# Second output projection, weight split and first routed tiles in one phase; routed tiles without a loop on TensorE

## The reference, cut to what matters

```python
# layer 0: 8 experts, 2 per token; layer 1: 16 experts, 4 per token
def step(acc, inputs):
    w1e, w2e, ce = inputs
    h = xt @ w1e                      # 256 -> 2 * 176
    a, b = jnp.split(h, 2, axis=-1)
    y = jax.nn.silu(a) * b @ w2e      # 176 -> 256
    return (acc + ce[:, None] * y, None)
...
out = jnp.einsum('bhqk,bkhd->bqhd', attn, V).reshape(B, S, D)
return out @ Wo.T + bo                # second output projection
```

## Time and profile before

| | |
|---|---|
| time, median of 3 runs | 2127.53 us |
| time of the profiled execution | 2133.09 us |
| its span | 2130.9 us |
| TensorE busy | 1723.5 us (81%), 10296 matmuls |
| VectorE, ScalarE, GpSimd busy | 1387.3, 946.3, 672.5 us |
| granted TensorE clock over the span | 0.92 of full speed |
| HBM read, written | 144.97 MB, 141.82 MB |

### The profile page before, as it was taken

The page is one execution under the profiler, slowest core; times in us unless marked ns, Lnnn a source line. Parts: engine busy times, 40 slices in busy tenths (PEclk is TensorE's granted clock), DMA queues, the critical chain, the costliest instruction groups (busy, mean ns, idle before and its releaser), DMA issues. The chain is left out here.

```text
span 2130.9 us, 36160 instructions
## 1 busy us (share of the span) xinstructions
PE 1723.5 (81%) x10296; PEld 1331.0 (62%) x10297; DVE 1387.3 (65%) x2825; ACT 946.3 (44%) x2201; POOL 672.5 (32%) x850
## 2 busy tenths in 40 slices
PE   3999985638892780899999999995688988879997
PEld 2877874428881560455555555543588888868886
DVE  4589996315564876977777777723455656546766
ACT  0455652313343651166666656663333434333343
POOL 1455621730006824044343434340000000027760
PEclk9999997869995895899999999998899999989999
DMA  6445523623333996235353535317633333356661
GB/s 224 156 125 172 152 43 84 223 87 96 104 99 119 321 352 191 69 97 134 93 138 90 145 82 148 82 49 208 187 96 103 103 99 110 99 177 191 200 191 53
DMA packets 288496, 292.61 MB, mean 137 GB/s; under 512 B 122665, under 2 KB 245034, under 8 KB 286300
## 3 DMA queue, kind: packets, MB, share of 16 engines
q1 hardware_dynamic: 265340, 236.62, 37.9%
q0 software_dynamic: 18432, 50.36, 7.5%
q10 hardware_dynamic: 4608, 4.20, 0.6%
HBM read 144.97 MB, written 141.82 MB: 135 GB/s over the span
## 5 line engine op out<-in xcount | busy, mean ns | idle before, releaser
L1473 ACT ACTIVATE ca_PT<-ca_psS 128x512 f32<-128x512 f32 (+3 forms) x768 | 344.9, 493 | 273.1 <-PE ca_psS L1508 259.7
L1399 DVE TENSOR_REDUCE ca_part<-ca_psM 128x1 f32<-128x512 f32 (+3 forms) x608 | 368.5, 656 | 85.3 <-PE ca_psM L1493 60.7
L1508 PE MATMUL ca_psS<-ca_QS,ca_KS 128*128 128x512 f32 (+3 forms) x768 | 306.1, 409 | 4.1 <-ACT ca_PT L1473 4.1
L801 POOL DMA_INDIRECT g_y<-ys_scratch,pos x128 | 130.7, 1021 | 501.9 <-POOLq L68 456.5
L1486 PE MATMUL ca_psM<-ca_KS,ca_QS 126*128 126x512 f32 (+3 forms) x768 | 247.1, 365 | 15.9 <-issue 13.7
L1508 PEld LDWEIGHTS ca_psS<-ca_QS,ca_KS 128*128 128x128 f32 x768 | 147.7, 195 | 106.4 <-ACT ca_PT L1473 101.3
L776 DVE TENSOR_TENSOR f_x_lo<-f_psT,f_x_hi 128x256 fp32r<-128x256 f32 x214 | 90.9, 425 | 162.2 <-ACT f_x_hi L755 157.6
L755 ACT ACTIVATE f_x_hi<-f_psT 128x256 fp32r<-128x256 f32 x214 | 82.3, 385 | 248.0 <-PE f_psT L708 247.7
L708 PE MATMUL f_psT<-ident,f_xs 128*128 128x128 f32 x428 | 89.2, 293 | 113.8 <-issue 56.9
L719 PE MATMUL f_psU<-ffn_hi,f_x_hi 128*128 x428 | 164.8, 385 | 1.0 <-DVE f_x_lo L776 1.0
L1486 PEld LDWEIGHTS ca_psM<-ca_KS,ca_QS 126*128 126x128 f32 x768 | 141.4, 194 | 37.4 <-DVE ca_part L1399 14.3
(11 more groups left out here) (258 smaller groups left out, 4386.6 us busy)
## 6 DMA issues: line engine op xcount, KB each, us to landing
f_xs<-xs_scratch SPq DMA_DIRECT2D x214, 128.0 KB, 2.0
ys_scratch<-f_ys SPq DMA_DIRECT2D x214, 128.0 KB, 1.7
xs_scratch<-fa_blank SPq DMA_DIRECT2D x32, 640.0 KB, 4.0
ca_QS<-qk_scratch SPq DMA_DIRECT2D x32, 512.0 KB, 6.7
ca_KS<-qk_scratch SPq DMA_DIRECT2D x32, 512.0 KB, 8.1
po_raw<-in_ffn SPq DMA_DIRECT2D x24, 608.0 KB, 4.8
xs_scratch<-fa_blank SPq DMA_DIRECT2D x32, 384.0 KB, 3.4
v_scratch<-gp_v_st SPq DMA_DIRECT2D x32, 256.0 KB, 3.8
```

The costliest lines, as they stand in the source:

```text
L801: pool.indirect_dma_start(dst[:, k, :], None, y_dram, bass.IndirectOffsetOnAxis(pos[:, tile, k:k + 1], 0)).then_inc(got, 16)
L1399: dve.tensor_reduce(dst, psM[(slot * NU + u) % SLOTS][:, 0:nh * w].rearrange("p (h k) -> p h k", h=nh), AX.X, ALU.max)\
L1473: act.activation(PT[:, s % 2, h, off:CHUNK], psS[(GH * s + h) % SLOTS][:, off:CHUNK], ACT.Exp)\
L1508: pe.matmul(psS[tile % SLOTS][:, off:CHUNK], KS[:, slot, h, kt * P:(kt + 1) * P], QS[:, slot, h, c * CHUNK + off:(c + 1) * CHUNK], start=T ...
```

## The change

1. `sparse_experts` (both layers use it before, the first layer after): TensorE's program is written out for all tiles instead of looping. `load_owners` is gone; `load_owner` loads one tile's expert number with one TENSOR_LOAD, once a step, between `up` and `transpose_h`. ScalarE, VectorE and SP keep their loops.
2. In the second layer `project_out` and `sparse_experts` are replaced by one phase, `project_beside_experts`. A step n, for n from 0 to 15, loads and splits expert n's weights, projects the attention's tiles 2n and 2n + 1, and carries the routed tiles, two steps later than the loads of the same step: `transpose` of tile n - 2, `up` of tile n - 3, `transpose_h` of n - 4, `down` of n - 5. From step 16 on only routed tiles are left. An `up` of one of the first 16 tiles waits for the split of the expert of its own number (a tile's expert never has a higher number). TensorE is written out here too; the others write out 24 steps and loop over the rest.
3. The projection's tiles have two staging buffers (`OB`) instead of four and share the PSUM buffers `psT` and `psY` with the routed tiles, which take turns in a fixed order (`turns_T`, `turns_Y`).
4. `mean_rstd`, `logits`, `before`, `every` and `tile_ids` are freed before this phase, which makes room for its buffers.

```diff
-def in_steps(eng, *stages, tiles=TILES, first=None, begin=None):
+def in_steps(eng, *stages, tiles=TILES, first=None, beside=None):
...
     whole = tiles // POS_TILES
-    if begin:
-        begin(0, first)
     for n in range(first):
+        if beside is not None:
+            beside(n)
         step(n)
     with eng.Fori(first // POS_TILES, whole) as b:
-        if begin:
-            begin(b * POS_TILES, POS_TILES)
         for i in range(POS_TILES):
             for lag, stage in stages:
                 back = -(-(lag - i) // POS_TILES) if lag > i else 0
                 stage(b * POS_TILES + (i - lag), (i - lag) % POS_TILES, b - back if back else b)
-    if begin:
-        begin(whole * POS_TILES, tiles + most - whole * POS_TILES)
     for n in range(whole * POS_TILES, tiles + most):
         step(n)
...
@@ -688,17 +684,11 @@
         def _(pe):
             owners = {}
 
-            def load_owners(n, count):
-                before = 0 if isinstance(n, int) and n == 0 else 3
-                count = min(count + before, NT - n + before) if isinstance(n, int) else count + before
-                _, values = nc.values_load_multi_w_load_instructions(te[0:1, bass.ds(n - before, count)], (pe.engine,), min_val=0, max_val=E - 1,
+            def load_owner(t, i, b):
+                _, values = nc.values_load_multi_w_load_instructions(te[0:1, t:t + 1], (pe.engine,), min_val=0, max_val=E - 1,
                                                                       skip_runtime_bounds_check_because="a count of ends, cut to E - 1 where it is written")
-                owners.clear()
-                owners.update({j - before: v for j, v in enumerate(values)})
-
-            def owner(i, lag):
-
-                return owners[(i + lag) % POS_TILES - lag]
+                owners.clear() if t == 0 else owners.pop(t - 4, None)
+                owners[t] = values[0]
 
...
             def up(t, i, b):
-                e = owner(i, 1)
+                e = owners[t]
...
             def down(t, i, b):
-                e = owner(i, 3)
+                e = owners[t]
...
                 ins.then_inc(down_done, 1)
-            in_steps(pe, (0, transpose), (1, up), (2, transpose_h), (3, down), tiles=NT, begin=load_owners)
+            for n in range(NT + 3):
+                for lag, stage in ((0, transpose), (1, up), (0, load_owner), (2, transpose_h), (3, down)):
+                    if lag <= n < NT + lag:
+                        stage(n - lag, (n - lag) % POS_TILES, (n - lag) // POS_TILES)
...
+def project_beside_experts(nc, tag, o_tile, s_dram, wo_dram, bo_dram, w_dram, E, NT, te, w_hi, w_lo, xs_dram, ys_dram, ident):
+
+    XR, YR, RAW, OB, SB = 4, 4, 2, 2, 4
+    LAG, PAIR = 2, TILES // E
+    FIRST = POS_TILES * -(-(E + 2) // POS_TILES)
+
+
+
+    def projected(n):
+        return range(PAIR * n, PAIR * (n + 1)) if 0 <= n < E else ()
...
+        h = sb("h", [P, 2, MID])
+        h_hi, h_lo = sb("h_hi", [HALF, 2, 2 * P], F32R), sb("h_lo", [HALF, 2, 2 * P], F32R)
+        wo, bo = sb("wo", [P, KT, HID]), sb("bo", [P, HID])
+        raw = sb("raw", [P, RAW, WE])
+        o_st, oT, s_sb = sb("o_st", [P, OB, HID]), sb("oT", [P, 2, HID]), sb("s_sb", [P, SB, HID])
+        psT, psU, psH, psY = ps("psT"), ps("psU"), ps("psH"), ps("psY")
+        wo_in, bo_in, oT_done, oT_out, s_done, s_out, hiw_done, low_done = (
...
+
+        turns_T, turns_Y = [], []
+        for n in range(NT + LAG + 4):
+            turns_T += [("o", t) for t in projected(n)] + [("x", n - LAG)] * (0 <= n - LAG < NT)
+            turns_Y += [("o", t) for t in projected(n - 1)] + [("x", n - LAG - 3)] * (0 <= n - LAG - 3 < NT)
+        place_T, place_Y = ({x: k for k, x in enumerate(turns)} for turns in (turns_T, turns_Y))
+        assert all(place[k, t] % 2 == t % 2 for place in (place_T, place_Y) for k, t in place if k == "x")
...
+            def beside(n):
+                if n >= E:
+                    return
+                if n >= RAW:
+                    sp.wait_ge(low_done, n - (RAW - 1))
+                sp.dma_start(raw[:, n % RAW, :], w_dram[n]).then_inc(raw_in[n % RAW], 16)
+                for t in projected(n):
+                    if t >= OB:
+                        sp.wait_ge(oT_done, t - (OB - 1))
+                    src = o_tile(t)
+                    sp.dma_start(o_st[:, t % OB, :].rearrange("p (g n) -> p g n", g=src.shape[1]), src).then_inc(staged[t % OB], 16)
+            sp.dma_start(wo[:], wo_dram).then_inc(wo_in, 16)
+            sp.dma_start(bo[:], bo_dram.partition_broadcast(P)).then_inc(bo_in, 16)
+            in_steps(sp, (0, load), (LAG + XR + 1, store), tiles=NT, first=FIRST, beside=beside)
+            for i in range(YR):
+                sp.wait_ge(stored[i], 16 * len(range(i, NT, YR)))
...
+            def load_owner(t, i, b):
+                _, values = nc.values_load_multi_w_load_instructions(te[0:1, t:t + 1], (pe.engine,), min_val=0, max_val=E - 1,
+                                                                      skip_runtime_bounds_check_because="a count of ends, cut to E - 1 where it is written")
+                owners.clear() if t == 0 else owners.pop(t - 4, None)
+                owners[t] = values[0]
+
+            def free(turns, at, x_out, o_out):
+                if at >= 2:
+                    kind, last = turns[at - 2]
+                    pe.wait_ge(x_out if kind == "x" else o_out, last + 1)
+
+            def transpose_o(t):
+                at = place_T["o", t]
+                pe.wait_ge(staged[t % OB], t // OB * 16 + 16)
+                free(turns_T, at, xlo_done, oT_out)
+                for k in range(KT):
+                    ins = pe.transpose(psT[at % 2][:, k * P:(k + 1) * P], o_st[:, t % OB, k * P:(k + 1) * P], ident[:])
+                ins.then_inc(oT_done, 1)
+
...
+            def transpose(t, i, b):
+                pe.wait_ge(x_in[i % XR], (t - i % XR) * 4 + 16)
...
+            def up(t, i, b):
+                e = owners[t]
+                pe.wait_ge(xlo_done, t + 1)
+                if t < E:
+                    pe.wait_ge(low_done, t + 1)
+                if late(t, 2):
...
+                ins.then_inc(down_done, 1)
+            pe.wait_ge(wo_in, 16)
+            for n in range(NT + LAG + 3):
+                for t in projected(n):
+                    transpose_o(t)
+                for t in projected(n - 1):
+                    project(t)
+                for lag, stage in ((LAG, transpose), (LAG + 1, up), (LAG, load_owner), (LAG + 2, transpose_h), (LAG + 3, down)):
+                    if lag <= n < NT + lag:
+                        stage(n - lag, (n - lag) % POS_TILES, (n - lag) // POS_TILES)
+
...
+            def keep(t):
+                act.wait_ge(s_out, t + 1)
+                act.dma_start(s_dram[t], s_sb[:, t % SB, :]).then_inc(kept[t % SB], 16)
+
+            def beside(n):
+                for t in projected(n):
+                    act.wait_ge(oT_done, t + 1)
+                    if t >= 2:
+                        act.wait_ge(s_done, t - 1)
+                    act.activation(oT[:, t % 2, :], psT[place_T["o", t] % 2][:, 0:HID], ACT.Copy).then_inc(oT_out, 1)
+                if n < E:
+                    act.wait_ge(raw_in[n % RAW], n // RAW * 16 + 16)
+                    act.activation(w_hi[:, n, :], raw[:, n % RAW, :], ACT.Copy).then_inc(hiw_done, 1)
+                for t in projected(n - 2):
+                    keep(t)
+            in_steps(act, (LAG, x_high), (LAG + 1, silu), (LAG + 2, h_high), tiles=NT, first=FIRST, beside=beside)
...
+            def beside(n):
+                for t in projected(n - 1):
+                    dve.wait_ge(s_done, t + 1)
+                    if t >= SB:
+                        dve.wait_ge(kept[t % SB], t // SB * 16)
+                    dve.tensor_tensor(s_sb[:, t % SB, :], psY[place_Y["o", t] % 2][:, 0:HID], bo[:], ALU.add).then_inc(s_out, 1)
+                if n < E:
+                    dve.wait_ge(hiw_done, n + 1)
+                    dve.tensor_tensor(w_lo[:, n, :], raw[:, n % RAW, :], w_hi[:, n, :].bitcast(F32), ALU.subtract).then_inc(low_done, 1)
+            dve.wait_ge(bo_in, 16)
+            in_steps(dve, (LAG, x_low), (LAG + 1, gated), (LAG + 2, h_low), (LAG + 3, take), tiles=NT, first=FIRST, beside=beside)
...
         ident = sb(top, "ident", [P, P])
-        mean_rstd = sb(top, "mean_rstd", [P, TILES, 2])
-        logits = sb(top, "logits", [P, TILES, RW1])
-        before, every = sb(top, "before", [P, P]), sb(top, "every", [P, P])
...
             ao_rows = ao_dram.rearrange("(b g) t p n -> b t p g n", g=GROUPS)
             w_hi, w_lo = sb(c, "ffn1_hi", [P, E1, WE], F32R), sb(c, "ffn1_lo", [P, E1, WE], F32R)
-            project_out(nc, "po1", lambda s, i: ao_rows[bass.ds(s, 1), i].rearrange("a p g n -> p (a g) n"), None, s1_dram,
-                        ident, a["wo1"], a["bo1"], 1.0, E1, a["ffn1"], w_hi, w_lo)
```

(11 more changed lines are left out.)

112 lines of the change are left out of this document (added).

## The result

The changed kernel takes **2041.64 us** (median of 4 runs, 2036.14 to 2042.87) beside 2126.98 us (2124.87 to 2137.63) of the kernel before on the same chip: a ratio of 0.9585, 95% interval 0.9556 to 0.9614, or 85.3 us less. The forecast was 2025 us, its range 2003 to 2175. The profiled executions are 97.0 us apart (2133.09 and 2036.14): that of before lies 6 us above its median, that of the change is the fastest of its four. The sum was made against the profiled execution of before.

A forecast was written before the change was run, and what follows sets the result against it. PE was taken to bound the second layer's routed tiles, transfers the projection before them. 29.0 us (first layer) plus 73.5 (second: 58.7 and 14.8) make 102.5, off 2133.1 gives 2030.6, forecast 2025 us after a 5.6 us median correction; range 2003 to 2175.

The forecast's parts named there:

- part 1: Routed tiles of both layers: writing TensorE out removes the boundary gaps and slow clock, saving 29.0 and 58.7 us, 87.7 together.
- the merging: Second layer: carrying routed tiles beside the second projection and expert splits saves 14.8 us.
- price of the new loads: Routed tiles: 214 one-value loads run beside queued matmuls and cost PE nothing; upper bound 0.85 us a tile.
- rival 1: Behind `up` in every tile: the load empties PE's queue, 0.85 us a tile, 172 us, total 2197 us; chance 0.23.
- Rival 2: Routed tiles: the sequencer becomes the bound, 2.35 us a tile, 44 us more, total 2070 us; chance 0.13.
- The forecast's own term: Routed tiles: sequencer needs 1.5 us to issue a tile plus 0.6 for a load, 2.1 us, just inside 2.13.
- length of the merged phase: Second layer: steps grow from 4.0 to 5.6 us, so weights are split 14 x 1.6 = 22.4 us later, at 1542.3.
- steady step: Merged phase: one expert, two projection tiles and a routed tile take 5.6 us a step.
- the staging buffers' round trip: Merged phase: with two staging buffers, load latency 4.7, issue 0.4 and transposes twice 0.3 give about 5.6 us a step.
- Rival 3: Merged steps take 8 us, projection transposes waiting for `x_low` behind the expert's low half; 34 us more, 2059 us; chance 0.06.
- bound by transfers: Merged phase: DMA ring time for a projection step and a routed tile sets steps of 4.9 us, total 2015 us.
- Rival 4: Routed tiles: the gap stays because other engines' loops cause as much; only the merging's 14.8 us remain, 2113 us; chance 0.03.

The follow-up runs named there:

- experiment 2: Kernel before with TensorE written out in both layers, phases unmerged, but eleven expert numbers loaded at every eighth tile: 2274.88 us, one run, ratio 0.981.
- experiment 4: Kernel before with its loops kept, one expert number loaded per tile behind `up` and three where a pass begins: ratio 0.9671.
- experiment 3: Kernel before with TensorE written out, phases unmerged, eight expert numbers per load at every eighth tile, none repeated: 2225.36 us, one run, ratio 0.960.
- experiment 11: The changed kernel with each tile's expert number loaded four times in a row, instead of once: 2248.70 us, one run.
- experiment 1: Kernel before with TensorE written out and one expert number loaded per tile in both layers, second layer's two phases unmerged: ratio 0.9622.

## Why the prediction was right, and where it wasn't

The time came out 16.6 us above the forecast, inside its range. Of the 102.5 us in the sum the two places gave 91.4: part 1 gave 90.6 where 87.7 were forecast, the merging 0.8 where 14.8 were.

**Part 1 was right in place and size.** Forecast 29.0 and 58.7 us, measured 28.7 and 61.9. The steps behind it hold one by one: the load starves PE (experiment 2), its length and not the loop is most of it (experiment 4), and the slow clock behind the gap is a third of a boundary's cost (1.0 to 1.1 of 3.45 us, experiment 2 and rows 1 to 3).

**The price of the new loads was rightly put at nothing.** The question was whether a load empties the queue. It doesn't, by experiment 3, and rival 1 falls. Rows 4 hardly told: 0.11 us where 0.2 was to be expected, between two loads. The sharper proof was out of reach before, since that trace has no load of eight values beside a busy PE. Rival 2 stood on the right mechanism. The sequencer can become the bound, but only from a second load a tile on: a load lasts 0.30 us (0.46 by what it adds to a tile), not 0.6 or 0.85. The forecast's own term, 1.5 + 0.6 = 2.1 of 2.13 us, thus looked tighter than it was (1.3 + 0.46, the estimate of experiment 11). The Trainium skill (DMA: Bandwidth & Descriptors, Latency and other measured facts) gives tensor_load a floor of about 600 ns. It isn't one here: the 214 loads of the change have a median of 0.303 us, the shortest take 0.296.

**The merging was forecast at 14.8 us and is worth none** (0.8 to 2.8 by the stretch, nothing by the ratio). The term that failed is the length of the merged phase. From the first weights' load to the last split it takes 1516.66 - 1416.72 = 99.9 us, and 1493.99 - 1426.77 = 67.2 unmerged: 32.7 more, not 22.4. Of these 10.3 us, 6 are the 13 steps from the third load to the last: 5.96 us on average instead of 5.6 (the early ones up to 7.3), beside 3.90 unmerged instead of 4.0. 4 are the last step, whose split comes 11.6 us behind its load and 7.8 unmerged, and 0.5 is the start. Most of what is left of the missing 14.0 is part 1, 3 us better than counted, which the merging can't save a second time. What it buys is fixed: 12 tiles, 25 us, and the gap between the phases, 8.

**The steady step came out right by luck.** 5.6 was taken from the staging buffers' round trip (whose terms, 4.7, 0.4 and 0.6, add up to 5.7), and 5.66 is the ring through psT's turns and `oT`. Rival 3 named half of that ring, `x_low` behind the expert's low half, but added a DMA's 4.7 us to it that is hidden. Neither looked at ScalarE's wait for `s_done`, which was there in the diff (`if t >= 2`). Tile t may be copied to `oT` only when tile t - 2 has been multiplied. In the phase before, that multiplication stands ahead of tile t's transposes in TensorE's program; in the change it stands behind the transposes of both tiles of the step, and the second's wait for `x_low`. Two `oT` buffers were enough for the one order and not for the other. With staging and `oT` at four the bound by transfers holds and the merging is worth 14 us after all (380.1 - 366.0). That this is near the 14.8 is luck too: by the prediction's sum steps of 4.9 us make it 24.6. Again part 1's 3 us, a longer last step (10.8 us from its load to the end of its split) and a longer start take most of the difference.

One reading of the prediction was loose without harm: rows 8 show the last work of the projection ending at 1519.82 + 0.75 = 1520.6; 1519.9 is where the last split ends, which is what the sum needs.

**Rival 4** falls with experiment 1. The loops of the other engines cost PE nothing that its waits show once TensorE's is gone, as forecast.

## What to carry to other kernels

Here a register load of the sequencer cost PE nothing while it ended before the queued work did; so look at how long such a load lasts, make it short (one value in every tile or eight in every eighth did equally well) and count the sequencer's time for a whole turn against the engine's. When two bound phases are merged, go round each ring of buffers in the new order, above all those that the diff takes over unchanged: a pair of buffers that was enough when a use stood ahead of the next fill isn't when it has moved behind it. A merged phase whose DMA share falls below that of the phase it replaces, as here from 0.93 to 0.73, is worth a look for such a ring.

## What was unexpected

The time of a TENSOR_LOAD doesn't follow its number of values: one takes 0.30 us, three 0.98, seven 1.33, eight 0.59, ten 2.56, eleven 2.85 (medians of experiments 2 to 4; for seven the longer of two loads, for ten the only one of experiment 2). The loads of three, seven, ten and eleven are the slow ones. Whether their count or where they start makes them slow wasn't tried.

An idle time of 1.64 us at every eighth tile left TensorE's granted clock at 0.99; one of 2.3 us in the same place went with 0.94, with 17 us more of busy time for the same matmuls.
